# ScalarE's order in a slot: the second gelu and its copy first, then the first gelu of half k+2

## The reference, cut to what matters

```
x = conv2d(x, conv1); residual = x
x = gelu(group_norm(x, gn1))            # the first gelu
x = conv2d(x, rconv1)
x = gelu(group_norm(x, gn2))            # the second gelu
x = residual + conv2d(x, rconv2)
x = conv2d(x, proj, stride 16)          # the projection to 192
```

## Time and profile before

| | us |
|---|---|
| median of 3 runs | 1846.43 (1845.34 to 1847.88) |
| the profiled execution | 1844.27 |
| its span | 1842.5 |
| busy in the span: PE, DVE, POOL, ACT | 1513.2, 1124.3, 884.6, 850.0 |
| loop over units: first and last second gelu begin | 285.7 and 1505.2 |

### The profile page before, as it was taken

One profiled execution on the slowest core, in us unless ns is written; L12 is line 12 of the kernel. 1 busy time (PEld: TensorE's weight loads), 2 busy tenths in 40 slices (PEclk: granted clock), 3 DMA queues, 4 the chain that ended last, 5 costly groups with the idle time before them and its releaser, 6 DMA issues. The chain is left out here.

```text
span 1842.5 us, 45180 instructions
## 1 busy us (share of the span) xinstructions
PE 1513.2 (82%) x13782; PEld 1018.5 (55%) x13782; DVE 1124.3 (61%) x4307; ACT 850.0 (46%) x2118; POOL 884.6 (48%) x2190
## 2 busy tenths in 40 slices
PE   6879967666888788878888887888788857788999
PEld 3434423333666466646665665566566647656657
DVE  8533437767766766767767766667667653347330
ACT  1212225665555555555555555555555530243441
POOL 2000026666666666656666666666666640123410
PEclk9989979999999999989999999999999988786999
DMA  5643353323444344334434443444344465700000
GB/s 163 197 115 92 94 198 82 79 72 98 113 122 108 99 126 117 98 106 112 122 92 116 124 114 84 122 113 120 94 116 122 115 165 158 159 1 1 1 1 14
DMA packets 117232, 190.78 MB, mean 104 GB/s; under 512 B 18251, under 2 KB 86282, under 8 KB 116940
## 3 DMA queue, kind: packets, MB, share of 16 engines
q1 hardware_dynamic: 117068, 188.60, 37.5%
HBM read 103.34 MB, written 21.30 MB: 68 GB/s over the span
## 5 line engine op out<-in xcount | busy, mean ns | idle before, releaser
L506 PE MATMUL rc<-sb_acts,sb_rwd 128*64 128x512 f16 x1764 | 565.8, 393 | 4.7 <-DMA sb_acts<-sb_hst 4.7
L507 PE MATMUL rc<-sb_acts,sb_rwd 128*64 128x512 f16 x1764 | 566.9, 394 | 0.0
L506 PE MATMUL rc<-sb_acts,sb_rwl 128*64 128x512 f16 x1176 | 368.3, 395 | 111.9 <-ACT sb_g2f L429 78.8
L420 ACT ACTIVATE sb_f32q<-c,sb_gsh,sb_gsc 128x128 f32<-128x128 f32 x792 | 298.6, 458 | 308.8 <-POOL sb_gsh L373 308.8
L429 ACT ACTIVATE sb_g2f<-rc,sb_gsh,sb_gsc 128x128 f32<-128x128 f32 x784 | 296.5, 469 | 216.7 <-POOL sb_gsh L373 202.3
L367 POOL TENSOR_TENSOR sb_tmp<-sb_tmp,sb_half_neg 128x4 f32<-128x4 f32 (+1 forms) x297 | 371.0, 1249 | 23.5 <-POOL sb_tmp L365 0.5
L507 PE MATMUL rc<-sb_acts,sb_rwl 128*64 128x512 f16 x1176 | 369.7, 396 | 0.0
L813 DVE TENSOR_TENSOR sb_arena<-sb_g2f,sb_arena 128x512 f32 (+1 forms) x196 | 135.8, 693 | 326.6 <-ACT sb_arena L437 313.1
L362 POOL TENSOR_TENSOR sb_tmp<-sb_mst 128x4 f32<-128x4 f32 (+1 forms) x297 | 71.6, 241 | 545.3 <-DVE sb_mst L793 545.2
L562 PE MATMUL pj<-sb_wall,sb_arena 128*64 128x384 f16 x1792 | 306.0, 339 | 20.4 <-DMA sb_wall<-w_lo 11.3
L566 PEld LDWEIGHTS pj<-sb_wall,sb_arena 128*64 128x64 f16 x1792 | 213.3, 225 | 72.3 <-issue 2.4
(11 more groups left out here) (161 smaller groups left out, 2310.2 us busy)
## 6 DMA issues: line engine op xcount, KB each, us to landing
sb_acts<-sb_hst SPq DMA_DIRECT2D x792, 78.8 KB, 2.1
sb_wall<-w_lo SPq DMA_DIRECT2D x56, 528.0 KB, 3.9
sb_im<-x_planes SPq DMA_DIRECT2D x202, 136.5 KB
sb_wall<-w_lo SPq DMA_DIRECT2D x28, 480.0 KB, 3.7
sb_f32q<-in_proj SPq DMA_DIRECT2D x12, 576.0 KB, 4.1
sb_arena<-in_proj SPq DMA_DIRECT2D x12, 576.0 KB, 4.4
w_lo<-sb_arena SPq DMA_DIRECT2D x1, 6144.0 KB, 17.3
scratch_fold<-sb_wall SPq DMA_DIRECT2D x48, 123.8 KB
```

What stands on the lines that cost most here:

```text
L420: ins = nc.scalar.activation(g1f[:, q * Q + m, :], c1[q][:, m * HALF:(m + 1) * HALF], ACT.Gelu, bias=gsh[q][:, m:m + 1], scale=gsc[q][:, m ...
L506: nc.tensor.matmul(out[0:CH, :], w_odd, x_odd, start=(n == 0), stop=(n == 14))
L507: yield nc.tensor.matmul(out[CH:128, :], w_even, x_even, start=(n == 0), stop=(n == 14))
```

## The change

In ACT's slot the two halves of the work trade places: `gelu2_at` and `hi2` of half k-3 are issued first, `gelu1` of half k+2 after them. No instruction is added or taken away, and no other engine's list changes. The wait on `s_pj` at the head of a group now stands before that slot's first gelu as well. The first three slots of the program still have only gelu1.

```
--- before.py
+++ after.py
@@ -443,15 +443,14 @@
                         u = u0 + p
                         for q in range(2):
 
+                            if not (first and 2 * p + q < 3):
+                                if head and 2 * p + q == 3:
+                                    act.wait_ge(s_pj, 1 if first else g)
+                                uu, qq, pp = (u - 2, 1, p) if q == 0 else (u - 1, 0, 1 - p)
+                                gelu2_at(uu, qq, pp)
+                                old = head and 2 * p + q < 3
+                                hi2(uu, qq, 1 - b if old else b, slot2(j, p, q, old))
                             gelu1(2 * u + 2 + q, q)
-                            if first and 2 * p + q < 3:
-                                continue
-                            if head and 2 * p + q == 3:
-                                act.wait_ge(s_pj, 1 if first else g)
-                            uu, qq, pp = (u - 2, 1, p) if q == 0 else (u - 1, 0, 1 - p)
-                            gelu2_at(uu, qq, pp)
-                            old = head and 2 * p + q < 3
-                            hi2(uu, qq, 1 - b if old else b, slot2(j, p, q, old))
```

## The result

The changed kernel takes 2241.41 us (2240.54 to 2254.49, 4 runs) against 1847.16 before (1845.34 to 1849.16, 4 runs). The ratio is 1.2151, with a 95% interval of 1.2104 to 1.2197. The forecast was 2260, with a range from 2120 to 2320. The profiled execution took 2242.01, with a span of 2240.2. Beside the experiments the kernel before was run again, at 1840.07 and 1839.52 (two medians of 11 runs), 0.4% less; their ratios are to these.

What follows compares the result with a forecast made beforehand. A ring of engines waiting for one another, 12.55 us a unit, bounds the kernel. 72 x (17.1 - 12.55) = 328 and 24 x 3.75 = 90 on the profiled 1844.3 make 2262; forecast 2260, range 2120 to 2320.

Steps and rivals of the forecast that it cites:

- The ring before: Odd slot: gelu2, hi2, DVE's split2, statistics, read of means, POOL's two norms, back to gelu2; 12.55 us a unit, no slack.
- Odd slot, the whole cost: ACT's odd slot: gelu1 moves behind gelu2, which needs POOL's second norm; 6.1 us later against 1.1 us of cover.
- Even slot, taken as 0 within 0 to 2.3: ACT's even slot: gelu1 delayed under 2.3 us behind gelu2 and hi2, not what ends last; effect taken as 0.
- the second read of the means: DVE reaches it 2.58 us after the first read; hidden inside POOL's first norm of 2.99, 0.4 us to spare.
- The new ring: From odd gelu2 by gelu1, conv1, PE's means and POOL's two norms to next gelu2: 15.7 us, 3.15 longer a unit.
- The clock: PE idles about 5 us before odd conv1, so its clock falls every unit; price 1.4 us, between 0 and 2.4.
- the smaller of its two rows: PE clock falls seen before the change: the single fall cost 1.45 us; the other row gives 2.4, half of 4.7.
- Units of group 0: Units without projection, 24 of 97 steps: 16.0 us forecast against 12.25 now, 3.75 more, including 1.5 for the clock.
- That the clock holds (2138): First rival: the ring lengthens by 3.15 us a unit with projection but PE's clock holds; 2138 us, chance 0.14.
- the reading that put the sum at most 21 us above that rival: Trainium skill page, part 1: PE's clock ramp is under 1% of a typical kernel and need not be modelled.
- The clock did not stay down through the loop: Second rival: PE's clock stays down through the loop and PE needs 21.8 us a unit; some 2630 us, chance 0.03.
- Nothing became faster: Third rival: odd gelu2 going first comes earlier and frees PE's tile, PE's waits go; 1690 us, chance 0.02.

## Why the prediction was right

*The ring before*, with gelu2 of the odd slot, hi2 and split2 on it and gelu1 beside it: right. The experiment with the later split2 took two links out of this chain, and the unit became about 1.1 us shorter (12.55 to 11.3 to 11.7), where 1.05 was expected of it.

*Odd slot, the whole cost*: right, by the run with that slot alone.

*Even slot, taken as 0 within 0 to 2.3*: as part of the change it held (2251 with the odd slot alone, 2241 with both). Alone it costs 36 us: the 0.4 us which the forecast gave the second read of the means as its spare are used up, and POOL's first norm, priced at 2.99, becomes longer as well.

*The new ring*: its path was right (conv1, the rest of PE's slot, means, two norms), its size not. At full clock it is 14.64 and not 15.7. The largest miss is POOL's second norm with 3.40 in place of 3.98, then 0.3 of ACT and its hand-over, where gelu1 ended at 3.66 and not at 3.8 and conv1 followed it by 0.05 and not by 0.2, and 0.2 of PE. POOL's durations were read in a unit in which DVE was probably in its way (below). The prediction had also said that the ring is wrong if a unit takes under 15 us at full clock. Units of 14.6 came. By that sign its length was wrong, while its other sign, a gelu2 of the odd slot that no longer waits for POOL, did not appear (9.72 and 9.98 us of waiting in the rows above).

*The clock*: the fall in every unit came as forecast, 97 of them. The price was too low, 2.3 to 2.6 in place of 1.4. (The eight idle times of 2.17 us or more that the forecast counted in the kernel before are nine, with seven falls.) The forecast had taken nearly the smaller of its two rows, on the ground that part of a low stretch would lie in the idle time. Here the low stretches are mostly longer too (628 us over 97, 6.5 each, as after the idle time of 4.12 in the earlier trace rows), so that the row of 2.4, which it had as the upper end, was the nearer one.

These two misses, -1.1 and about +1.1, cancel almost exactly. That the sum is within 1% of the measured time is luck; its terms are not that good. Units of group 0, which has no projection, took 15.4 on average (16.0 and 14.8 in turn) where 16.0 was forecast.

*Rivals.* That the clock holds (2138) is refuted by the granted clock, and with it the reading that put the sum at most 21 us above that rival. That the run with 32 filler matmuls took 2138.62 is a coincidence: the clock fell in 64 of its 97 steps. The rival's own ring was also too long: at full clock throughout it would be near 1845 + 72 x 2.1 + 24 x 1.85 = 2040, an estimate which no run reached. The clock did not stay down through the loop. Nothing became faster, for the reason given: ACT waits for the second norm whatever stands in front.

## What to carry to other kernels

Before two pieces of work trade places on an engine, ask of each what it waits for and who waits for it. A piece that was ready early and stood ahead of a long wait had the wait as its cover; put behind it, it brings the wait to everyone who needs it. An engine that is busy 46% can still have its order on the ring. And when a change makes TensorE's idle time long and puts it in one place, count its clock in: here the falls of the clock after 97 idle times of 4 to 5 us cost some 200 us (2241 less the estimate of 2040), and giving PE useless work won a part back.

## What the runs showed of the hardware

*TensorE's clock.* An idle time of 4.06 us in front of conv1 was followed by 1.2 GHz for 5.1 us of work. With the filler of 32, 2.2 to 2.4 us of idle were left in front of conv1 in most units, and the clock fell in 64 of 97 steps. With 40 matmuls 1.7 to 1.9 were left, and it fell in 35.

*POOL beside DVE.* One operation of the second norm, 128 x 8 elements, takes 620 ns in the kernel before and 205 ns in the changed one, with the same operands. POOL's groups by shape, from 700 to 1400 us, before and then after (line, engine, operation, tiles, shape, count, busy, mean ns, idle before):

```profile
L367 POOL TENSOR_TENSOR sb_tmp<-sb_tmp,sb_half_neg 128x8 f32<-128x8 f32 x55 | 96.4, 1752 | 4.5 <-POOL sb_tmp L365 0.3
L369 POOL TENSOR_TENSOR sb_gsc<-sb_tmp,sb_wid 128x8 f32<-128x8 f32 x55 | 34.1, 620 | 4.3
```

```profile
L367 POOL TENSOR_TENSOR sb_tmp<-sb_tmp,sb_half_neg 128x8 f32<-128x8 f32 x42 | 68.8, 1639 | 3.5 <-POOL sb_tmp L365 0.3
...
L369 POOL TENSOR_TENSOR sb_gsc<-sb_tmp,sb_wid 128x8 f32<-128x8 f32 x42 | 8.6, 205 | 3.3
```

In the kernel before, this operation ran from 1011.24 to 1011.91, and DVE's split of fp32 and fp16 from 1011.15 to 1011.84; they end within 0.07:

```profile
1011.24 0.67 POOL L369 TENSOR_TENSOR sb_gsc<-sb_tmp,sb_wid 128x8 f32<-128x8 f32 x1
```

The Trainium skill ("SBUF — State Buffer", the section on the two separate sides) says that a DVE operation with two inputs in SBUF and a GpSimd operation that reads SBUF exclude each other for the whole instruction. The rows agree with it. Over the whole trace of the kernel before, 92 of the 98 operations of this line and shape took more than 0.3 us and ended 0.05 to 0.07 us after split1's second operation (DVE L806, 128 x 512, two inputs in SBUF). Of the four that took less, and of all 98 in the changed kernel, none overlapped with a DVE operation of that kind. No run here moved that one operation alone, so it stays the likely cause and not a shown one.

Of the changed kernel's 72 units with projection 63 come out between 16.8 and 17.3, though some of them have more to project. That was seen and not explained.
